# A linear-attention and routed-expert layer: x loaded ahead of the weights, squared weights summed in bf16, and the scale worked out by halves

## The reference

```python
qkv = xn @ w_attn.T                      # 16 heads of 16, phi = elu + 1 on q and k
num = (mask * (q k^T)) v + q S           # by chunks of 128 tokens
den = row sums of mask * (q k^T) + q z
S, z = S + k^T v, z + sum of k
attn = (num / (den + 1e-6)) @ w_proj.T
expert = argmax(xn @ gate_w.T + gate_b + expert_bias)
ffn = relu(xn @ w1[expert] + b1[expert]) @ w2[expert] + b2[expert]
```

## Time and profile before

| | |
|---|---|
| median of 3 runs | 521.93 us |
| the three runs | 519.39, 521.93, 522.41 us |
| the profiled execution | 522.73 us |
| its span, first to last instruction | 520.9 us |
| mean granted clock of TensorE | 0.971 of full |
| busy: PE, DVE, ACT, POOL | 484.3, 405.9, 279.2, 271.6 us |
| end of the attention loop's first product to the first expert product | 23.33 to 298.87 us |

### The profile page before, as it was taken

How to read it: one execution, slowest core, us unless ns; L and a number is a source line. 1 busy time by engine, 2 the same in 40 slices (tenths; PEclk the granted TensorE clock), 3 DMA queues, 4 the chain that set the end, 5 groups by cost and what they waited for, 6 DMA issues and landing times.

```text
span 520.9 us, 17449 instructions
## 1 busy us (share of the span) xinstructions
PE 484.3 (93%) x6071; PEld 395.8 (76%) x6071; DVE 405.9 (78%) x885; ACT 279.2 (54%) x535; POOL 271.6 (52%) x469
## 2 busy tenths in 40 slices
PE   4489999999999999999997499999999999999996
PEld 1378888788887888778875388888888888888884
DVE  2778889999899998999878547767768676677775
ACT  0346888788778787878885033333333333333331
POOL 3444766667766677766754533443534534433322
PEclk9679999999999999999998789999999999999999
DMA  8413556566466565573452431222122212220000
GB/s 272 156 57 99 164 172 211 162 190 202 154 205 179 175 205 179 159 223 129 161 166 102 142 93 62 69 66 79 59 63 72 66 57 82 63 69 23 28 15 1
DMA packets 34160, 62.88 MB, mean 121 GB/s; under 512 B 5661, under 2 KB 10014, under 8 KB 33952
## 3 DMA queue, kind: packets, MB, share of 16 engines
q1 hardware_dynamic: 29088, 49.17, 29.7%
q0 software_dynamic: 4992, 12.60, 8.0%
HBM read 51.00 MB, written 13.50 MB: 124 GB/s over the span
## 4 chain that ended last, share of the span: by engine, by line
PE 82%; DVE 5%; POOL 4%; issue 4%; ACT 3%; DMA 2%; DVEq 0%; POOLq 0%; ACTq 0%
PE ps L601 20%; PE ps L614 20%; PE ps L376 7%; PE ps L416 6%; PE ps L445 5%; PE ps L486 5%; PE ps L459 4%; PE ps L429 3%; PE ps L392 3%; PE ps L472 2%; PE ps L570 2%; PE ps L399 1%; PE ps L359 1%; PE ps L349 1%; PE ps L478 1%
## 5 line engine op out<-in xcount | busy, mean ns | idle before, releaser
L601 PEld LDWEIGHTS ps<-AR,W 128*128 x1872 | 131.6, 99 | 40.0 <-issue 1.1
L601 PE MATMUL ps<-AR,W 128*128 128x128 f16 x1872 | 155.9, 221 | 0.9 <-ACT AR L1148 0.9
L614 PE MATMUL ps<-W,ST 128*128 x624 | 150.4, 326 | 0.3 <-DVE ST L1008 0.3
L1157 ACT ACTIVATE ST<-ST 128x512 f16<-128x512 f32 x78 | 49.2, 630 | 112.0 <-DVE ST L996 107.3
L996 DVE SCALAR_TENSOR_TENSOR ST<-ps,TAs,B1S 128x512 f32<-128x512 f32 x78 | 58.4, 748 | 51.5 <-PE ps L601 48.3
L1305 POOL DMA_INDIRECT out<-AR x39 | 39.8, 1021 | 103.9 <-DVE AR L1028 99.6
L1245 POOL TENSOR_TENSOR W<-ST,W 128x512 f16<-128x512 f32 x64 | 74.3, 1161 | 28.8 <-ACT W L1107 28.1
L713 DVE TENSOR_TENSOR AR<-ps,CT 128x512 f32<-128x512 f32 x128 | 82.0, 683 | 4.4 <-PE ps L416 4.2
L1300 POOL DMA_INDIRECT AR<-scr,AR x39 | 49.9, 1279 | 34.6 <-issue 14.3
L1008 DVE SCALAR_TENSOR_TENSOR ST<-ST 128x512 f16<-128x512 f32 x78 | 53.6, 687 | 15.7 <-ACT ST L1157 15.3
L376 PE MATMUL ps<-xT,WA 128*128 128x128 f16 x768 | 50.7, 225 | 3.1 <-ACT xT L1057 3.1
(11 more groups left out here) (149 smaller groups left out, 765.9 us busy)
## 6 DMA issues: line engine op xcount, KB each, us to landing
ST<-in_w SPq DMA_DIRECT2D x128, 256.0 KB, 4.2
scr<-XR SPq DMA_DIRECT2D x32, 256.0 KB, 2.2
XR<-in_x SPq DMA_DIRECT2D x32, 128.0 KB, 4.6
AR<-in_b SPq DMA_DIRECT2D x1, 1024.0 KB, 5.0
AR<-in_wall SPq DMA_DIRECT2D x1, 776.0 KB, 4.5
AR<-scr,AR POOLq DMA_INDIRECT x39, 3.6
out<-AR POOLq DMA_INDIRECT x39
ST<-in_cst SPq DMA_DIRECT2D x1, 576.0 KB, 4.9
```

The lines of the kernel that those rows point to most:

```text
L601: a = e.matmul(dst, W[:, off:off + 57472][:, bass.ds(place_of(s), 128)], XT16[s % 2][:, xl * 256 + k * 128:xl * 256 + (k + 1) * 128], star ...
L614: a = e.matmul(PS[4 + s % 2][:, 0:w], src[h % 4][:, fs], W[:, off:off + 57344 + w][:, bass.ds(place_of(s), w)], start=(f == 0 and w == 512 ...
L1157: e.activation(HH[h % 4], H32[h % 2], ACT.Relu).then_inc(a_hh, 1)
```

## The change

- `sync` issues x of chunks 0 and 1 first, then `WF` in its two halves with a semaphore each, then the constants.
- The squares are written in bf16. `vector` squares half 0 behind the statistics of chunks 0 and 1, `scalar` squares half 1 with ACT's Square. `tensor` sums with the bf16 ones `one16`, 388 columns at a time, in banks 3 and 4, now one tensor of 1024 columns.
- `vector` normalises chunk 0 (`nb(0)`) ahead of everything that works out the scale. One reduction over both banks takes the place of two and a maximum, and four instructions on the bits take the place of eight; the second scale comes one instruction behind the first, with a second step of `v_sv`.
- The high and the low part of the weights are made in two pieces: columns 0 to 511 of both halves (q and k), in step 0 behind `xh(0)`, and columns 512 to 775 in step 1 behind `xTc(0)`. `qk(0)` waits for the first, `vg(0)` for the second.
- `gpsimd` fills `one16` first, and copies the identity behind the roots of chunks 0 and 1.

```diff
         def sync(e):
-            e.dma_start(WF, wall).then_inc(d_wall, 16)
             load_x(0)
+            load_x(1)
+            for k in range(2):
+                e.dma_start(WF[:, k, :], wall[:, k, :]).then_inc(d_wall[k], 16)
             e.dma_start(CT[:, :], cst).then_inc(d_cst, 16)
-            load_x(1)
...
-                    e.wait_ge(v_wa, 1)
+                    e.wait_ge(v_wa, 2)
                     e.dma_start(RST, cst2).then_inc(d_cst2, 16)
         def tensor(e):
-            e.wait_ge(p_ones, 1)
-            e.wait_ge(v_sq, 1)
-            for n0, n1, bank in ((0, 512, 3), (512, 776, 4)):
-                for k in range(2):
-                    a = e.matmul(PS[bank][:, 0:n1 - n0], ONF, SQ[:, k, n0:n1], start=(k == 0), stop=(k == 1))
+            e.wait_ge(p_one16, 1)
+            for k in range(2):
+                if k == 0:
+                    e.wait_ge(v_sq, 1)
+                else:
+                    e.wait_ge(a_sq, 1)
+                for i in range(2):
+                    a = e.matmul(PS[3 + i][:, 0:388], one16[:, :], SQ[:, k, i * 388:(i + 1) * 388],
+                                 start=(k == 0), stop=(k == 1))
             a.then_inc(t_sq, 1)
             def vg(c):
+                if c == 0:
+                    e.wait_ge(v_wa, 2)
...
                 if p == 2:
                     e.wait_ge(v_bmd, 1)
+                    e.wait_ge(p_ones, 1)
         def vector(e):
-            e.wait_ge(d_wall, 16)
-            e.tensor_tensor(SQ, WF, WF, ALU.mult).then_inc(v_sq, 1)
...
             na(1)
+            e.wait_ge(d_wall[0], 16)
+            e.tensor_tensor(SQ[:, 0], WF[:, 0], WF[:, 0], ALU.mult).then_inc(v_sq, 1)
+            nb(0)
+
             e.wait_ge(t_sq, 1)
-            e.tensor_reduce(nv[:, 0:1], PS[3][:, :], X_AX, ALU.max)
-            e.tensor_reduce(nv[:, 1:2], PS[4][:, 0:264], X_AX, ALU.max).then_inc(dv.up(), 1)
...
+            e.tensor_reduce(nv[:, 0:1], PSS[3][:, :].rearrange("p (i n) -> p i n", i=2)[:, :, 0:388], AX_XY,
+                            ALU.max).then_inc(dv.up(), 1)
             e.wait_ge(dv.sem, dv.n)
+            e.tensor_scalar(nv[:, 1:2], nv[:, 0:1], 2.0 ** -107, 2.0 ** 113, ALU.max, ALU.min).then_inc(dv.up(), 1)
             e.wait_ge(dv.sem, dv.n)
+            e.tensor_scalar(ni[:, 0:1], nv[:, 1:2].bitcast(I32), -0.5, 204.5 * 2 ** 23,
+                            ALU.mult, ALU.add).then_inc(dv.up(), 1)
             e.wait_ge(dv.sem, dv.n)
+            e.tensor_scalar(SV[:, 0:1], ni[:, 0:1], EXP, None, ALU.bitwise_and).then_inc(v_sv, 1)
+            e.wait_ge(v_sv, 1)
+            e.tensor_scalar(SV[:, 1:2], SV[:, 0:1], -1.0, 244.0 * 2 ** 23, ALU.mult, ALU.add).then_inc(v_sv, 1)
-            nb(0)
-            e.wait_ge(a_wa, 1)
-            e.scalar_tensor_tensor(WA[:, 1, :, :], WF, sv(0), WA[:, 0, :, :], ALU.mult, ALU.subtract).then_inc(v_wa, 1)
+            for i, n in enumerate((slice(0, 512), slice(512, 776))):
+                e.wait_ge(a_wa, i + 1)
+                e.scalar_tensor_tensor(WA[:, 1, :, n], WF[:, :, n], sv(0), WA[:, 0, :, n],
+                                       ALU.mult, ALU.subtract).then_inc(v_wa, 1)
         def scalar(e):
-            e.wait_ge(v_sv, 1)
-            e.activation(WA[:, 0, :, :], WF, ACT.Copy, scale=sv(0)).then_inc(a_wa, 1)
+            e.wait_ge(d_wall[1], 16)
+            e.activation(SQ[:, 1], WF[:, 1], ACT.Square).then_inc(a_sq, 1)
+
+            def wa_hi(n):
+                e.activation(WA[:, 0, :, n], WF[:, :, n], ACT.Copy, scale=sv(0)).then_inc(a_wa, 1)
...
                 if on(p - 1):
                     xTc(p - 1)
+                if p == 1:
+                    wa_hi(slice(512, 776))
...
                     xh(p)
+                if p == 0:
+                    e.wait_ge(v_sv, 1)
+                    wa_hi(slice(0, 512))
                 if on(p - 1):
+                    if p == 1:
+                        e.wait_ge(v_sv, 2)
                     relu(p - 1)
         def gpsimd(e):
+            e.memset(one16[:, :], 1.0).then_inc(p_one16, 1)
             e.memset(ONF, 1.0).then_inc(p_ones, 1)
-            e.wait_ge(d_cst, 16)
-            e.tensor_copy(id16[:, :], cc(C_ID, 128)).then_inc(p_id, 1)
...
                 if p == 0:
                     nn_end(1)
+                    e.wait_ge(d_cst, 16)
+                    e.tensor_copy(id16[:, :], cc(C_ID, 128)).then_inc(p_id, 1)
                 if p == 1:
...
-                    e.memset(one16[:, :], 1.0)
                     e.wait_ge(t_sq, 1)
-                    e.memset(ON2, 1.0).then_inc(p_one16, 1)
+                    e.memset(ON2, 1.0).then_inc(p_ones, 1)
```

More of the change, by code:

```diff
@@ L12 @@
 X_AX = mybir.AxisListType.X
+AX_XY = mybir.AxisListType.XY
 B, T, D = 4, 1024, 256
@@ L75, in sem @@
             return ctx.enter_context(nc.semaphore(name))
-        PS = [ctx.enter_context(nc.psum_tensor(f"ps{i}", [128, 512], F32)) for i in range(8)]
+        PSS = {i: ctx.enter_context(nc.psum_tensor(f"ps{i}", [128, 1024 if i == 3 else 512], F32))
+               for i in (0, 1, 2, 3, 5, 6, 7)}
+        PS = [PSS[i][:, 0:512] if i != 4 else PSS[3][:, 512:1024] for i in range(8)]
         W = sb("W", [128, E * 8192], F16)
@@ L111, in program @@
         ni = sb("ni", [128, 4], I32)
-        SI = sb("SI", [128, 2], I32)
         SV = sb("SV", [128, 2], I32)
@@ L139, in program @@
         WF = ar(0, 1552).rearrange("p (k n) -> p k n", k=2)
-        SQ = ar(1552, 1552).rearrange("p (k n) -> p k n", k=2)
+        SQ = ar(1552, 776, BF16).rearrange("p (k n) -> p k n", k=2)
         ONF = ar(3200, 128)
@@ L257, in program @@
         d_scr = [sem(f"d_scr{i}") for i in range(R)]
-        d_wall, d_wp, d_cst, d_tri, d_small, d_cst2, d_b2 = (
-            sem(n) for n in ("d_wall", "d_wp", "d_cst", "d_tri", "d_small", "d_cst2", "d_b2"))
+        d_wall = [sem(f"d_wall{k}") for k in range(2)]
+        d_wp, d_cst, d_tri, d_small, d_cst2, d_b2 = (
+            sem(n) for n in ("d_wp", "d_cst", "d_tri", "d_small", "d_cst2", "d_b2"))
         d_wm = [sem(f"d_wm{i}") for i in range(4)]
@@ L266, in program @@
         t_bmx, v_bmd, t_bma, v_eb1 = (sem(n) for n in ("t_bmx", "v_bmd", "t_bma", "v_eb1"))
-        v_sq, t_sq, v_sv, a_wa, v_wa, v_bm = (sem(n) for n in ("v_sq", "t_sq", "v_sv", "a_wa", "v_wa", "v_bm"))
+        v_sq, a_sq, t_sq, v_sv, a_wa, v_wa, v_bm = (sem(n) for n in ("v_sq", "a_sq", "t_sq", "v_sv", "a_wa", "v_wa", "v_bm"))
         names = ("sums", "na", "nn", "nb", "xh", "xl", "xt", "xTc", "qk", "relu", "exp", "phi", "km", "sc", "pv", "ktr", "kt",
@@ L494, in place @@
                     e.wait_ge(p_tri, 1)
-                    e.wait_ge(p_one16, 1)
                 n = min(8 * g + 12, NC)
@@ L519, in mxa @@
                 if ex == 0:
-                    e.wait_ge(p_one16, 1)
+                    e.wait_ge(p_ones, 2)
                 e.matmul(PMA, ON2, MMD[:, ex, :], start=True, stop=True).then_inc(t_mxa, 1)
@@ L667, in vector @@
             e.wait_ge(dv.sem, dv.n)
-            e.tensor_tensor(nv[:, 2:3], nv[:, 0:1], nv[:, 1:2], ALU.max).then_inc(dv.up(), 1)
+            e.tensor_scalar(nv[:, 1:2], nv[:, 0:1], 2.0 ** -107, 2.0 ** 113, ALU.max, ALU.min).then_inc(dv.up(), 1)
             e.wait_ge(dv.sem, dv.n)
-            e.tensor_scalar(ni[:, 0:1], nv[:, 2:3].bitcast(I32), 23, None, ALU.logical_shift_right).then_inc(dv.up(), 1)
+            e.tensor_scalar(ni[:, 0:1], nv[:, 1:2].bitcast(I32), -0.5, 204.5 * 2 ** 23,
+                            ALU.mult, ALU.add).then_inc(dv.up(), 1)
@@ L671, in vector @@
             e.wait_ge(dv.sem, dv.n)
[L672 to L678, removed]
@@ L679, in vector @@
-            e.tensor_scalar(SI[:, 1:2], ni[:, 0:1], 39.0, None, ALU.add).then_inc(dv.up(), 1)
-            e.wait_ge(dv.sem, dv.n)
-            e.tensor_scalar(SV[:, :], SI[:, :], 23, None, ALU.logical_shift_left).then_inc(v_sv, 1)
-            nb(0)
-            e.wait_ge(a_wa, 1)
-            e.scalar_tensor_tensor(WA[:, 1, :, :], WF, sv(0), WA[:, 0, :, :], ALU.mult, ALU.subtract).then_inc(v_wa, 1)
+            e.tensor_scalar(SV[:, 0:1], ni[:, 0:1], EXP, None, ALU.bitwise_and).then_inc(v_sv, 1)
```

## The result

The changed kernel took 514.65 us (median of 4 runs, 513.84 to 514.76) against 520.69 for the kernel before in the same comparison; the ratio is 0.9878, 95% interval 0.9846 to 0.991. That is inside my range of 514.5 to 519.0, by 0.15 us, but the gain is 1.2%, where I had called "within 1%" the likelier side by a hair. The gain is 6.0 us between the medians, and I had worked out 5.3. The four runs of the kernel before lie apart, 519.39 and 519.46 against 521.93 and 522.41, and their median falls between the two pairs, so the 6.0 depends on how many of each were drawn.

What follows compares the result with a forecast made beforehand. PE, busy 93% of the span, was taken as the bound, so moving phi(0) moves the end. phi(0) from 24.77 to 19.45 gains 5.3 us; the median 521.93 less 5.3 gives 516.6 us, range 514.5 to 519.0.

Steps and rivals of the forecast that it cites:

- x in front: First loads: x(0), issued at 0.74, is there at 3.84 us, bounds 3.3 and 5.2.
- Squares and roots: POOL's roots wait while DVE squares its half of the weights, running 6.2 to 10.04; ending 9.2 without that stall.
- The identity's copy: POOL's copy behind the roots goes ahead of DVE's nb(0): 0.28 us lost, bounds 0 and 0.28.
- The sums: PE's bf16 sums of squares end at 8.3; the 4.1 us saved become waiting for the roots.
- The scale and the copies: DVE reduction nearly 1.0 us, v_sv at 12.35, ACT's first half 1.09, DVE's subtraction 1.25, qk(0) at 14.8.
- The give-back at relu(0): ACT makes x(1)'s high part before relu(0): 0.45 us lost; 0.5 of qk(0)'s gain given back at phi(0).
- The clock: TensorE's clock rise moves with the work at no cost; bounds up to 0.8 us either way.
- (a): Rival: loads no quicker for being first, x(0) at 5.24; gain 3.9, 518.0 us, chance 0.14.
- (d): Rival: change ineffective or swallowed by a wait beyond phi(0), loop keeps its old times; 521.9 us, chance 0.05.
- (b): Rival: roots escape the squares or loads come at 2.6; gain 6.2 to 6.5, 515.6 us, chance 0.16.
- (c): Rival: Square needs a second ACT table load, 1.28 us between qk(0) and phi(0); gain 4.0, 517.9 us, chance 0.04.
- (e): Rival: slower, clock rise comes whole chunks later; three chunks too late gives 528.6 us, chance 0.03.

Runs made afterwards that it cites:

- e3: Changed kernel with both halves of the weights' squares on ACT, none on DVE: 514.54 us, phi(0) at 17.20.
- e11: Changed kernel with the identity's copy ahead of the roots on POOL, as before the change: median 517.42 us, phi(0) at 20.11.
- e2: Changed kernel with the squares and their sums in float32: median 516.93 us, phi(0) at 19.42.
- e7: Kernel before the change with only the squares and their sums in bf16: median 516.70 us, phi(0) at 20.66.
- e5: Kernel before the change, unchanged, profiled a second time: span 517.5 us, phi(0) at 23.49.
- e8: Changed kernel, unchanged, profiled and timed again: median 513.75 us, span 511.2, phi(0) at 18.15.
- e10: Changed kernel with 50 products of ones by ones on PE in the wait for the first gathered tokens: median 514.49 us.
- e6: Kernel before the change with only x of chunks 0 and 1 issued ahead of the weights: ratio 1.0016, phi(0) at 25.76.
- e1: Changed kernel with the weights' two halves issued ahead of x again: median 518.05 us, phi(0) at 20.45.
- e9: Changed kernel with products of ones by ones where PE stands idle ahead of the loop: median 514.63 us, phi(0) at 17.92.
- e13: Changed kernel with 70 products of ones by ones in PE's idle stretches behind the last qk: median 513.33 us, span 511.0.
- e14: Changed kernel with both squares on ACT and 70 products of ones by ones behind the last qk: median 512.37 us, span 510.3.
- e12: Changed kernel with the weights' high and low parts each made in one instruction of 1552 columns: median 515.63 us, phi(0) at 18.70.

## Why the prediction was right or wrong

**x in front: the step that failed.** "Bounds for x(0): 3.3 and 5.2; I take the row of the same size, 3.84." It landed at 2.90, outside the bounds. The row was a load in the running loop; the first two loads of the program, 128 KB each with nothing ahead of them, took 2.1 us each. That is 0.94 of the 1.5 us by which phi(0) came earlier than forecast. The rest is 0.1 in the roots, 0.3 at the identity's copy and 0.1 in the reduction. With x alone put right the sum is 6.2 us, 1.2%, where 5.3 had left it on the 1% line and the likelier call on the wrong side of it. My own sign of being wrong, phi(0) before 18.6, came true. That the time still fell inside the range is no merit of this step: the range held it by 0.15 us.

**Squares and roots: right in kind.** I had 0.85 us of hold and measured 0.74 (e3). Not in the order I described: the roots began at 4.41, before the weights were there, and were caught in the middle. The Trainium skill's rule ("SBUF — State Buffer", section "SBUF: two separate sides") of an exclusive lock, which it gives for a DVE instruction with two inputs in SBUF beside a POOL one that reads SBUF, is borne out by that step, 0.93 beside the squares and 0.19 without. ACT's half of the squares ended at 7.32, and not before 7, at no cost.

**The identity's copy: wrong.** "I let POOL come first: 0.28 us lost; bounds 0 and 0.28." POOL did come first, by 0.10 us, and nothing was lost: 0.29 of copy and 0.41 of `nb(0)` overlap. So not each DVE instruction on SBUF is held by a POOL one, and the lower bound was the right one. The larger point I missed: I priced this edit at its hold, while undoing it costs 2.2 us (e11).

**The sums: half right.** They did become a wait, DVE stood 2.57 us for the roots. But I wrote that 4.1 us saved become waiting, as though the saving were lost; e2 shows 1.5 us of it on the path, and e7 that alone it gives 4.1 at phi(0) against a profile with slow sums, 2.8 against one with faster ones.

**The scale and the copies: right.** The reduction 0.96, three steps to 10.84, 1.15 and 1.14 to 1.28 for the first pieces, against 1.0, 0.57, 1.09 and 1.25. From the first `v_sv` on, qk(0) came 2.65 us later, where I had 2.45. The give-back at relu(0) was forecast as 0.5 in all and measured 0.26: qk(0) gained 7.09 us and phi(0) 6.83.

**The clock: the mechanism was named, its size was not.** "I let the rise move with the work, at no cost. Bounds: 1.5 us of low clock more or less, up to 0.8 us either way." Two executions of the unchanged kernel differ by 2.8 us at qk(4), 2.6 of it through the clock, and the stretch behind the last qk by up to 2.2 between kernels. I had worked from an execution of the later rise and from a median of the same group, and so compared like with like only by luck. The first spans of the two kernels lie 8.1 us apart, e5's and e8's 6.3, and e5's and the changed kernel's first 4.7; none of these is the gain, the ratio over many runs is. I took the distance from qk(1) to qk(4) as 22.9 us from a piece of the chain; by the first products it is 22.7, and 22.3 in the changed kernel, within the 1 us that I had allowed.

**Rivals.** (a) and (d) fell with x at 2.90 and with qk(4) 7.2 us earlier. (b), earlier loads, is what happened, though not through roots that escaped; its figure of 6.2 to 6.5 does not follow from loads of 2.6 us alone, which by my own sum give 5.8. (c) fell: ACT has one table load, 1.28 us at 0.73, and Square lives with exp. (e) did not occur: the rise came within qk(1)'s chunk.

**Open.** Why e10's faster first products gave nothing; why the clock falls behind the last qk in some executions and not in others with the same idle stretch; and how much of a median over four runs is which group.

## What to carry to other kernels

At a start, list what each engine's first instruction waits for, and take the parts together: x in front was worth nothing alone (e6) and 2.5 us here (e1), because before the change the path ran through the weights and their sums and not through x; and it would have been worth little with the identity's copy still ahead of the roots (e11). For a load at the start take a duration from a load at a start, not from the running loop. Before a gain of 1% is forecast or believed, see how far two profiles of the same kernel lie apart, stretch by stretch, and look at the stretches where PE idles.

## What the runs showed of the hardware

- The granted clock reads 1.00 at the start of a profile although PE works at the low rate. In the profile after:

```profile
13.40:20.00 6.60, 5.57 (x39) 1.00 0.90 306
20.00:26.00 6.00, 5.50 (x48) 1.00 0.18 58
```

  In these stretches 24 products took 2.72 and 2.74 us, the 1.2 GHz level, against 1.51 later. In the kernel before it reads 1.00 from 0 to 15 us, where the float32 sums took 5.51 us. At the start durations tell, the column does not.
- Products of ones by ones raised the clock ahead of qk(0) (e9: 24 products in 1.50 us against 2.72). With them behind the last qk it stayed at full until 282 in e13 and the stretch was at its shortest (33.8 and 33.9 us) in e13 and e14, as it was in two of 14 profiles without.
- The first two loads of 128 KB, issued at 0.74 and 1.18, landed 2.1 us after their issue (2.0 and 2.8 in e8), against 4.5 for the same size issued second behind 776 KB.
- An 8x8 instruction of DVE (L692 in the kernel before) took 0.92 us where it started just behind POOL's product of 512 columns (25.68 and 25.54 in the kernel before, 19.61 and 19.47 in e12) and 0.24 where it started ahead of it (18.85 and 19.03 in the changed kernel).
